# Half-position scans on one Trainium2 core: where GpSimd's states lie, when VectorE weighs, and drives made in pairs

## What is computed

```python
def step(h, inp):
    dtt, ut, bt, ct = inp
    dA = jnp.exp(dtt[..., None] * A)
    h = h * dA + (dtt * ut)[..., None] * bt[:, :, None, :]
    y = jnp.einsum('bkdn,bkn->bkd', h, ct)
    return (h, y)
```

## Time and profile before

| what | us |
| --- | --- |
| median of three runs | 5606.2 |
| lowest and highest of them | 5602.42, 5620.28 |
| the profiled execution's own time | 5607.85 |
| its span, first to last instruction | 5606.0 |
| granted TensorE clock, mean | 0.945 of full |

### The profile page before, as it was taken

How to read it: one execution, slowest core, us unless ns; L and a number is a source line. 1 busy time by engine, 2 the same in 40 slices (tenths; PEclk the granted TensorE clock), 3 DMA queues, 4 the chain that set the end, 5 groups by cost and what they waited for, 6 DMA issues and landing times. The chain is left out here.

```text
span 5606.0 us, 73119 instructions
## 1 busy us (share of the span) xinstructions
PE 4828.6 (86%) x23205; PEld 3411.3 (61%) x23205; DVE 4445.6 (79%) x4529; ACT 3634.0 (65%) x5725; POOL 3960.4 (71%) x3074
## 2 busy tenths in 40 slices
PE   7888797789898887888989888888998988888998
PEld 5776546656666645555666645565666654556777
DVE  6889838959999848977999957996999975896544
ACT  5666455448887757767878857775878865775222
POOL 5888619839999818857999935894999962984111
PEclk9999999989999998998999999998999999999999
DMA  5777607737877616647788724654877842562110
GB/s 206 263 252 264 211 10 258 252 132 254 287 268 268 226 34 219 224 135 250 260 280 271 269 69 171 220 183 161 281 266 276 271 166 102 201 216 93 43 43 29
DMA packets 356676, 1104.83 MB, mean 197 GB/s; under 512 B 33210, under 2 KB 121126, under 8 KB 354872
## 3 DMA queue, kind: packets, MB, share of 16 engines
q1 hardware_dynamic: 356280, 1100.06, 56.9%
HBM read 1086.24 MB, written 13.68 MB: 196 GB/s over the span
## 5 line engine op out<-in xcount | busy, mean ns | idle before, releaser
L1157 PE MATMUL banks<-ident,prod 128*128 128x128 f32 x4752 | 764.9, 287 | 392.5 <-DVE prod L1458 286.6
L1157 PEld LDWEIGHTS banks<-ident,prod 128*128 128x128 f32 x4752 | 556.8, 145 | 799.1 <-DVE prod L1458 557.8
L1449 DVE TENSOR_TENSOR_SCAN banks<-banks,h 128x512 f32<-128x512 f32 x594 | 723.3, 1218 | 85.8 <-ACT banks L1297 48.5
L1400 POOL TENSOR_TENSOR h<-lane,Bb 128x512 f32<-128x512 f32 x576 | 722.8, 1272 | 57.8 <-DMA Bb<-half_rows 33.8
L1297 ACT ACTIVATE banks<-lane,A 128x512 f32<-128x512 f32 x864 | 581.1, 686 | 251.6 <-DVE prod L1458 82.4
L1229 PE MATMUL banks<-w_a,Cb 128*128 128x384 f32 x1536 | 552.2, 488 | 0.0
L1449 DVE TENSOR_TENSOR_SCAN banks<-banks,half_carry_a,h 128x512 f32<-128x512 f32 x396 | 505.5, 1277 | 8.8 <-ACT banks L1297 4.9
L1400 POOL TENSOR_TENSOR h<-half_du_a,Bb 128x512 f32<-128x512 f32 x384 | 482.7, 1275 | 14.8 <-DMA Bb<-half_rows 10.1
L1297 ACT ACTIVATE banks<-half_delta_a,A 128x512 f32<-128x512 f32 x576 | 385.3, 685 | 151.5 <-DVE lane L1430 73.7
L1217 PE MATMUL banks<-big,w_a 128*128 128x256 f32 x1728 | 435.0, 394 | 1.0 <-DMA w_a<-w_in 0.8
L1458 DVE TENSOR_TENSOR prod<-banks,half_C_a 128x512 f32<-128x512 f32 x528 | 365.3, 692 | 73.4 <-DMA half_C_a<-half_rows 2.4
(11 more groups left out here) (471 smaller groups left out, 12291.6 us busy)
## 6 DMA issues: line engine op xcount, KB each, us to landing
Bb<-half_rows SPq DMA_DIRECT2D x576, 512.0 KB, 4.3
C_first<-rows SPq DMA_DIRECT2D x288, 512.0 KB, 5.4
Cb<-half_rows SPq DMA_DIRECT2D x288, 512.0 KB, 4.4
w_a<-w_in SPq DMA_DIRECT2D x256, 576.0 KB, 6.1
w_b<-w_in SPq DMA_DIRECT2D x128, 576.0 KB, 6.2
half_C_a<-half_rows SPq DMA_DIRECT2D x128, 512.0 KB, 6.7
Bb<-rows SPq DMA_DIRECT2D x96, 512.0 KB, 5.5
half_C_b<-half_rows SPq DMA_DIRECT2D x64, 512.0 KB, 6.6
```

The lines of the kernel that those rows point to most:

```text
L1157: mm = eng.matmul(ps[:, 0, at], src[:, at], m.ident[:, :], start=n == 0 and k == 0, stop=added(s) == (i + 1) * N, is_transpose=True, skip_ ...
L1400: eng.tensor_tensor(m.dBu[:, s % DRIVES, :], m.du[i % 2], m.B[b % BRING][:, cols(s % 2)], ALU.mult).then_inc(st.dbu, 1)
L1449: eng.tensor_tensor_scan(flip(to), flip(slot(s)), flip(m.dBu[:, s % DRIVES, :]), initial, ALU.mult, ALU.add).then_inc(st.scanned, 1)
```

## The change

Five things are changed, all in `fused_scans` and in the tiles that it is given.

- The five states that GpSimd weighs are now 0, 3, 6, 9 and 12 of a lane, and their decay is written by ScalarE straight to a `held` tile in SBUF. They take no PSUM bank. The scan reads the decay and writes its output in that same tile; ScalarE, not VectorE, waits until the tile was added.
- VectorE weighs a state of its own behind the scan of the next state, and TensorE adds it one step later.
- GpSimd makes the drives of two states in one 128 x 1024 instruction, with `du` repeated. The ring is two pairs where it was three single tiles; pair b is made when the scans of pair b - 2 are done, and a scan waits for its whole pair.
- `du` is made at step 12 of a lane, and ahead of the drive of that step.
- Some steps of guests move by one, and one 128 x 512 tile is added.

```diff
-    SLOTS, DRIVES, PRODS, HELD, BRING = 4, 3, 3, 3, 3
+    SLOTS, DRIVES, PRODS, HELD, BRING = 4, 2, 3, 3, 3
+    POOLED = (0, 3, 6, 9, 12)
...
-    BEHIND = 2
-    GATE_AT, PRODUCT_AT, OUT_AT, OUT_COPY_AT = 9, 6, 9, 11
+    BEHIND, DU_AT = 2, 12
+    GATE_AT, PRODUCT_AT, OUT_AT, OUT_COPY_AT = 9, 7, 9, 11
...
-    INPUT_AT, INPUT_PLACE_AT, INPUT_TAKE_AT = 6, 9, 11
+    INPUT_AT, INPUT_PLACE_AT, INPUT_TAKE_AT = 7, 9, 11
...
     def by_pool(s):
-        return s % N % 3 == 1
+        return s % N in POOLED
...
-        places.append(("step", step))
+        if not by_pool(step):
+            places.append(("step", step))
...
     def slot(s):
-        return bank("step", s)
+        return held[pooled(s) % HELD] if by_pool(s) else bank("step", s)
...
-                    eng.wait_ge(st.dbu, s - 2 * BRING + 2)
+                    eng.wait_ge(st.dbu, b - BRING + 1)
...
+                if s and s <= STEPS and not by_pool(s - 1):
+                    add(s - 1)
                 if s < STEPS:
-                    if not by_pool(s):
-                        add(s)
...
-                    if i + 1 < LANES and n == DELTA_AT - 4:
+                    if i + 1 < LANES and n == DELTA_AT - 3:
                         dt_product(i + 1)
...
-                vacated(eng, "step", s)
+                if not by_pool(s):
+                    vacated(eng, "step", s)
+                elif pooled(s) >= HELD:
+                    eng.wait_ge(st.summed, added(pool_steps[pooled(s) - HELD]))
...
-            def drive(s):
-                i, n = s // N, s % N
-                b = s // 2
-                if n == 0:
+            def drive(b):
+                i = b // PAIRS
+                if b % PAIRS == 0:
                     eng.wait_ge(st.du, i + 1)
                 eng.wait_ge(st.b[b % BRING], 16 * (b // BRING + 1))
-                if s >= DRIVES:
-                    eng.wait_ge(st.scanned, s - DRIVES + 1)
-                eng.tensor_tensor(m.dBu[:, s % DRIVES, :], m.du[i % 2], m.B[b % BRING][:, cols(s % 2)],
-                                  ALU.mult).then_inc(st.dbu, 1)
+                if b >= DRIVES:
+                    eng.wait_ge(st.scanned, 2 * (b - DRIVES + 1))
+                eng.tensor_tensor(m.dBu[b % DRIVES], over_tiles(m.du[i % 2], 2),
+                                  m.B[b % BRING].rearrange("p (r l) -> p r l", r=2), ALU.mult).then_inc(st.dbu, 1)
...
+            drive(0)
             for s in range(STEPS):
                 i, n = s // N, s % N
-                drive(s)
+                if n == DU_AT and i + 1 < LANES:
+                    du(i + 1)
+                if n % 2 == 0 and s + 2 < STEPS:
+                    drive(s // 2 + 1)
                 if n >= BEHIND and by_pool(s - BEHIND):
                     weigh(s - BEHIND)
-                if n == 14 and i + 1 < LANES:
-                    du(i + 1)
...
-                eng.wait_ge(st.dbu, s + 1)
-                to, initial = slot(s), 0.0
+                eng.wait_ge(st.dbu, s // 2 + 1)
+                initial = 0.0
...
-                if by_pool(s):
-                    if pooled(s) >= HELD:
-                        eng.wait_ge(st.summed, added(pool_steps[pooled(s) - HELD]))
-                    to = held[pooled(s) % HELD]
-                eng.tensor_tensor_scan(flip(to), flip(slot(s)), flip(m.dBu[:, s % DRIVES, :]), initial,
+                eng.tensor_tensor_scan(flip(slot(s)), flip(slot(s)), flip(m.dBu[s // 2 % DRIVES][:, s % 2, :]), initial,
                                        ALU.mult, ALU.add).then_inc(st.scanned, 1)
...
                 if s < STEPS:
                     scan(s)
-                    if not by_pool(s):
-                        weigh(s)
+                if s and s <= STEPS and not by_pool(s - 1):
+                    weigh(s - 1)
+                if s < STEPS:
...
-                             dBu=m.h[:, 0:2, :].rearrange("p a (b n) -> p (a b) n", n=HALF)[:, 0:3, :],
-                             held=m.h[:, 1:3, :].rearrange("p a (b n) -> p (a b) n", n=HALF)[:, 1:4, :],
+                             dBu=[m.h[:, k, :].rearrange("p (r l) -> p r l", r=2) for k in range(2)],
+                             held=[m.h[:, 2, cols(0)], m.h[:, 2, cols(1)], named_more],
```

More of the change, by code:

```diff
@@ L884, in own @@
         return s - pooled(s)
-    lane_order = [a for b in range(N) for a in ([] if by_pool(b) else [b]) +
+    lane_order = [a for b in range(N + 1) for a in ([b - 1] if b and not by_pool(b - 1) else []) +
                   ([b - BEHIND] if b >= BEHIND and by_pool(b - BEHIND) else [])]
@@ L922, in lane @@
         return directions[d], i % TILES, c
-    held = [m.held[:, b, :] for b in range(HELD)]
+    held = m.held
     prods = [m.prods[:, b, :] for b in range(PRODS)]
@@ L937, in fused_scans @@
     evicts = {pair_at(v, 2) + 3: (v + 1) * 2 // PER - 1 for v in range(PAIRS_IN) if (v + 1) * 2 % PER == 0}
-    LAST = max([STEPS] + [s + 7 for s in evicts])
+    LAST = max([STEPS + 1] + [s + 7 for s in evicts])
     def chunk(k):
@@ L981, in fused_scans @@
             until = place_of["step", b] + SLOTS
-            keeps.setdefault(max(s for s in range(b, b + SLOTS + 1) if place_of["step", s] <= until), []).append(b)
+            keeps.setdefault(max(s for s in own_steps[own(b):own(b) + SLOTS + 1] if place_of["step", s] <= until), []).append(b)
     def vacated(eng, what, k):
@@ L1000, in vacated @@
             eng.wait_ge(st.x_taken, b + 1)
-        elif by_pool(b):
-            eng.wait_ge(st.scanned, b + 1)
         else:
@@ L1151, in add @@
                     eng.wait_ge(st.prod, own(s) + 1)
-                if n == 0 and i:
+                if n == lane_order[0] and i:
                     eng.wait_ge(st.copied, i)
@@ L1156, in add @@
                     at = slice(k * P, (k + 1) * P)
-                    mm = eng.matmul(ps[:, 0, at], src[:, at], m.ident[:, :], start=n == 0 and k == 0,
+                    mm = eng.matmul(ps[:, 0, at], src[:, at], m.ident[:, :], start=n == lane_order[0] and k == 0,
                                     stop=added(s) == (i + 1) * N, is_transpose=True, skip_group_check=True)
@@ L1254, in _ @@
                         turn_residual(turned_of[i])
-                if s == STEPS - 1:
+                if s == STEPS:
                     back(LANES - 1)
@@ L1275, in magnitude @@
                 if i >= 2:
-                    eng.wait_ge(st.dbu, (i - 1) * N)
+                    eng.wait_ge(st.dbu, (i - 1) * PAIRS)
                 eng.activation(m.du[i % 2], bank("delta", i), ACT.Abs).then_inc(st.magnitude, 1)
@@ L2816, in half_scan_tensors @@
                     (f"half_carry_{name}", [P, DT1 * N], F32),
-                    (f"half_delta_{name}", [P, HALF], F32), (f"half_du_{name}", [P, HALF], F32)])
+                    (f"half_delta_{name}", [P, HALF], F32), (f"half_du_{name}", [P, HALF], F32),
+                    (f"half_more_{name}", [P, HALF], F32)])
                 named = {key[5:-len(name) - 1]: t for key, t in made.items()}
+                named_more = named["more"][:, :]
                 named = dict(low=low_0, C=rows_C, carry=named["carry"], delta=[delta_0, named["delta"][:, :]],
```

## The result

The changed kernel takes 5940.86 us (median of four runs, 5932.75 to 5952.63) against 5608.84 us before: a ratio of 1.0591, 95% interval 1.0564 to 1.0619. It is slower by 5.9%, 332 us; 5915 was forecast, in a range of 5640 to 6090.

The account below looks back on a forecast made before the run. VectorE's queue was taken as the bound, within 2 us of GpSimd's. With exclusion a lane takes 32.9 us, 2.85 over 30.1; 108 lanes add 308 us to 5607.85, or 5916, stated as 5915; range 5640 to 6090.

Parts of the forecast that it names:

- The exclusion: In five scans with both operands in SBUF: each holds GpSimd off 1.14 us (1.08 in first halves) and waits for it.
- Rival A: At the scans of states 0, 3, 6, 9, 12: they don't exclude GpSimd; about 5435 us, chance 0.16.
- The saving of the weighing: In VectorE's queue: each of eleven products behind the next scan saves 0.21 us, 2.3 us a lane.
- rival C: At VectorE's products: the SBUF scans exclude GpSimd and weighing later saves nothing; 34.5 us a lane, 6080 us, chance 0.04.
- the freed banks: PSUM banks no longer used by GpSimd's five states: four banks span nearly six steps, covering ScalarE; costed at nothing.
- Drives in pairs: In GpSimd's queue: a pair takes 2.37 us against two of 1.27, so eight pairs 18.6 where sixteen drives were 19.7.
- the hand rules: Both queues written out by instruction, with overlaps, waits and exclusion: 31.7 us in first halves, 33.3 in second.
- The lane: One lane of the six half-position scan stages: 32.9 us on average after the change, 2.85 more than 30.1.
- the evictions: 96 evictions in VectorE's queue, 0.53 us each, 0.47 a lane on average; 0.4 was added to the lane after.
- GpSimd's copies of a carry: In first halves: five copies with their wait add about 1.0 us, taken to fall beside VectorE's holds.
- a random moment of asking: At the SBUF scans: a scan asking at random waits 1.05 us for the rest of a GpSimd instruction.
- the unexplained 0.5 us a lane: Kernel before: the rules with evictions give 29.6 us a lane against 30.1 measured; half was said to be hidden after.

Follow-up runs that it names:

- short drives: The changed kernel with GpSimd's pairs of drives cut to the first 32 of each 512 columns: 5370.8 us, ratio 0.9579.

## Why the prediction was right, step by step

**The exclusion** was the step that decided, and it held: the SBUF scans' durations and the three rows in order of time above are the earlier trace rows over again, the run with this part alone costs 302 us against 332 for all, putting the decays back in banks takes 310 away, and with short drives the long scans are gone. Rival A would have been 5435. No run has the changed kernel's full queues and its freed banks without exclusion; with short drives, where GpSimd's queue is much shorter too, it takes 5371.

**The parts** add up along one path: decays in SBUF alone +302 (5909), pairs on top +175 (6084), weighing behind the next scan -143 (5941). Along another, the weighing is worth 58 (5909 to 5850) and the pairs cost 90. The sizes depend on each other; what they end at does not. One thing more changes along both paths: the run with decays in SBUF alone has GpSimd weigh the states 1, 4, 7, 10 and 13, the others 0, 3, 6, 9 and 12. So the 175 and the 58 hold that move as well, while the 143 is of the weighing alone and the 90 of the pairs with their ring and the earlier `du`.

**The saving of the weighing** is real (rival C is out): 0.24 for each product where 0.21 was forecast, and 143 us arrive of 249 by the forecast and 285 by the measured 0.24. The Trainium skill, "VectorE: DVE Perf Modes", section "The DRAIN you can't avoid", says that leaving out the semaphores between VectorE operations gains nothing. The rows of the run with this part alone show 1.19 for 1.40, and they decide it for this kernel. What I missed is what the saving needs. I costed the freed banks at nothing, with ScalarE's lead as the cover to name. They pay for the weighing: with banks for all and single drives, it loses 48 us instead.

**Drives in pairs** cost 2.36 in the median, as taken. That single drives would give the same lane under exclusion, as the hand rules had it, was too kind to pairs, by 90 us.

**The lane** came out at 33.3 for a forecast of 32.9, right in the mean but not in its halves. By the starts of its scans the changed kernel takes 33.9 us in lanes of a first half and 32.8 in those of a second; I had 31.7 and 33.3, and with 0.4 for the evictions 32.1 and 33.7. Three lanes of a first half and the three of the second that follow, by window:

```profile
core 0: us, PE busy (x) PEld busy (x) DVE busy (x) ACT busy (x) POOL busy (x), PEclk, DMA share, GB/s
1624.50:1728.50 104.00, 86.90 (x396) 61.01 (x396) 91.22 (x92) 72.19 (x127) 89.22 (x57) 0.90 0.68 232
1728.50:1826.30 97.80, 85.13 (x397) 61.37 (x398) 90.94 (x90) 70.88 (x101) 88.34 (x44) 0.91 0.72 250
```

The same three and three lanes of the run with the product right behind its scan:

```profile
1645.10:1745.90 100.80, 85.33 (x395) 60.29 (x395) 90.59 (x92) 71.47 (x126) 89.45 (x58) 0.92 0.70 237
1745.90:1850.20 104.30, 87.38 (x401) 60.07 (x400) 99.21 (x91) 72.08 (x103) 81.29 (x43) 0.93 0.71 234
```

Over all lanes that run takes 33.9 us in first halves and 34.9 in second. So weighing behind the next scan saves 2.1 of the forecast 2.3 us in second halves, and nothing in first halves. The term that I mis-sized is the saving in first halves, which I had at 2.3. The other two pairs of runs that differ in the weighing lean the same way: from the kernel before to weighing behind only, first halves lose 1.3 and second halves keep their time; with decays in SBUF and single drives, where GpSimd's states move too, first halves lose 0.1 and second halves gain 0.8.

Two things are seen in first halves, and no run separates them. I let GpSimd's copies of a carry fall beside VectorE's holds; but a copy reads SBUF too:

```profile
1700.35 1.96 DVE L1449 TENSOR_TENSOR_SCAN half_more_a<-half_more_a,h 128x512 f32<-128x512 f32 x1
...
1701.17 1.11 POOL L1410 COPY half_carry_a<-h 128x1 f32<-128x1 f32 x1
...
1702.36 1.27 POOL L1412 TENSOR_TENSOR h<-h,half_C_a 128x512 f32<-128x512 f32 x1
```

It takes 1.11 us for 0.18, up to the end of the scan. 87 of the 270 copies take over 0.5 us, and all together 126 us where the kernel before has 50; with the product right behind its scan it is 22 copies and 70 us. The other thing is ScalarE's own copies of carries. Such a copy comes after the product of its state, and the bank is not free before it. ScalarE's waits there in the first stage, in the kernel before and in the changed one:

```profile
ACT half_carry_a L1289 <- DVE prod L1458: 24.5, 32, 1.6
```

```profile
ACT half_carry_a L1289 <- DVE prod L1458: 62.5, 38, 5.0
```

With weighing behind only, where no copy of GpSimd's is held, these waits are 57.4 us and the first halves still lose. So the held copies are not needed for it; that ScalarE's waits are the cause is argued from these rows and not shown by a run of its own.

**The scans' durations.** The forecast of a median above 1.8 for the SBUF scans held for one form, 1.96, and not for the others, 1.64 to 1.72: the waits are less even than a random moment of asking makes them. Pairs of 3 to 3.7 us were forecast; there are many over 3, and none over 3.31.

**How near the number is** is partly luck. With the evictions, the first halves came out 1.8 over the forecast and the second 0.9 under it, and the two cancel by half. The sum also says that half of the unexplained 0.5 us a lane is hidden, but 32.9 has none of it in; with half, it would be 33.15 and about 5936. And the forecast had nothing move outside the stages, where 18 us were gained. One reading was off without weight in the sum: that neither queue waits 2 us for the other in the two lanes of the earlier trace rows. GpSimd waits there for VectorE for 3.2 us:

```profile
POOL h L1410 <- DVE h L1449: 2.1, 4, 1.0
...
POOL h L1400 <- DVE banks L1449: 1.1, 1, 1.1
```

## What to carry to other kernels

Look at where both operands of a VectorE instruction lie before taking a tile out of PSUM: in this kernel, beside a busy GpSimd, a second SBUF operand made VectorE wait for what GpSimd had begun, and held GpSimd for nearly the length of the scan. Five such scans of sixteen cost 302 of 5607 us. A ring of banks is shortened by every instruction that lets go later, so move work behind other work where the next user of the bank is quick, and count the banks before moving all of it. Weighing behind the next scan was worth 1.1% once it was applied to five states of eleven and the rest was left as it was, where all eleven lost 0.9%.

## What was not expected of the hardware

A 128 x 1 copy on GpSimd, 0.18 us alone, is held to the end of a scan like a long instruction (1.11 us). A scan with both operands in SBUF takes 1.21 us while GpSimd reads little, the same as with one in PSUM, so nothing in a profile with an idle GpSimd would warn of it. A product of 0.69 us is recorded as 0.67 when it follows a scan it doesn't wait for, and lets the next scan start at 0.58 to 0.59 instead of 0.61.
